# Second product of the expert layer with the activations stationary, in a fused decoder layer

## The chip, the cores and the metric

The kernel runs on one core of a Trainium2 chip. The metric is the device time of one execution in microseconds (us). TensorE is called PE (its weight loads PEld), VectorE DVE, ScalarE ACT, GpSimd POOL and SyncE SP, as in the profile.

## The reference, cut to what matters

The layer takes x of shape (8, 128, 128): 1,024 tokens of width 128. A bidirectional Mamba mixer, a cross attention and a mixture of experts follow one another, each with a residual and a layer norm. All is float32. The change lies in the experts:

```
logits = tokens @ gate_w                       # 8 experts
expert_idx = argmax(softmax(logits))           # top 1
pos = cumsum(one_hot(expert_idx)) - 1          # place in the expert's queue, capacity 160
expert_input = einsum('tec,td->ecd', sec_mask, tokens)     # (8, 160, 128)
h = relu(einsum('ecd,edf->ecf', expert_input, w1))         # (8, 160, 512)
expert_output = einsum('ecf,efd->ecd', h, w2)              # (8, 160, 128)
out = einsum('tec,ecd->td', combine_weights, expert_output)
```

## The kernel before, in words

Every engine has a program of its own, written out by hand, and they meet at semaphores. PE's results go to the 8 PSUM banks of 128 x 512 float32. A list, `plan` (lines 210 to 237), names every result in the order in which PE makes it, with the bank that it goes to; from it come the waits: `to_fill` waits until what stood in the bank was read, `filled` tells that it is full, `to_read` waits for that, `was_read` tells that it was copied out.

The mixer takes the first 240 us or so, attention the next 75. The experts are the last stage. POOL writes each token row to its slot in DRAM (`dispatched_tokens`, line 475, 8 indirect transfers), SP loads the 1,280 slots back as `xe` (lines 355 and 356), PE turns them to `xeT` (width on partitions, slots along the row; line 994, carried out in the helper `turn`, line 687), ACT and DVE copy that out of PSUM. Then comes the loop over 8 experts with 160 slots each, in steps `e` of PE's program (lines 997 to 1018):

- `h{e}`: the first product, 4 matmuls of 128 x 160 with a block of w1 stationary and the slots of `xeT` moving (line 1002). It fills a pair of banks, 0 and 1 or 2 and 3. ACT copies it out with a relu, to `hid`, two buffers in turn (line 680); before that it waits until the second product has read the buffer (line 678).
- `eoT{e-1}`: the second product of the expert before, 4 matmuls accumulated over the 512 hidden units with a block of w2 stationary and `hid` moving, 160 columns (line 1010). The result has the width on partitions. It goes to bank 4 or 5; DVE copies it to `eoT` (line 1293, in the helper of line 1032).
- `eo{e-2}`: two transposes of 80 slots each (line 1017, helper line 687) put the slots on partitions: 80 x 2 x 128, in bank 6 or 7. DVE copies that to `eo` (line 1296, the same helper).

SP stores `eo` to DRAM in pairs of experts once both are copied (line 362). POOL waits for all four stores and fetches each token's row with 8 indirect transfers (line 481); DVE weighs it, adds the residual and normalizes (lines 1301, 1174, 1175, 1180), and SP stores the output.

A float32 matmul has two LDWEIGHTS and two MATMUL records in the trace, a transpose one of each.

Of the kernel before, what the change touches and what calls it, by code (L numbers as in the profile page):

```python
# [22 lines left out]
def decoder_layer_kernel(nc, x, ctx_1024, in_proj_w, conv_w, conv_bias, x_proj_w, dt_proj_w, dt_proj_bias,  # L23
                         A_log, D_skip, convb_w, convb_bias, x_proj_b_w, dt_proj_b_w, dt_proj_b_bias,
                         A_b_log, D_b_skip, out_proj_w, Wq, Wk, Wv, Wo, gate_w, w1, w2, out):
    B, S, D = x.shape
# [25 lines left out]
    E = gate_w.shape[1]  # L52
    F = w1.shape[2]
    FC = F // P
    CAP = 160
    HC = CAP // 2
# [9 lines left out]
    with ExitStack() as ctx:  # L66
        def sb(name, shape, dt=F32):
            return ctx.enter_context(nc.sbuf_tensor(name, shape, dt))
# [25 lines left out]
        w2_sb = sb("w2_sb", [P, E, FC, D])  # L94
# [20 lines left out]
        arena = sb("arena", [P, 12, T])  # L115
# [47 lines left out]
        x2T = arena[:, 9, :]  # L163
        xe = arena[:, 0:2, :].rearrange("p a t -> p (a t)")[:, 0:SLOTS].rearrange("p (j d) -> p j d", j=ST)
        xeT = arena[:, 2:4, :].rearrange("p a t -> p (a t)")[:, 0:SLOTS]
        eoT = [arena[:, 9, CAP * k:CAP * k + CAP] for k in range(2)]
        hid = [arena[:, 4 + e, 0:FC * CAP].rearrange("p (c s) -> p c s", c=FC) for e in range(2)]
        eo = arena[:, 6:8, :].rearrange("p a (e s d) -> p (a e) s d", s=2, d=D)
        back = arena[:, 10, :].rearrange("p (b d) -> p b d", b=B)
# [40 lines left out]
        plan = [("xT0", 0), ("xT1", 1), ("winT", 2), ("wkT0", 3), ("xi0", 5), ("xi1", 6), ("xproj", 7), ("dtw", 2)]  # L210
# [20 lines left out]
                plan += [("x2T0", 0), ("logits0", 1)]  # L231
        plan += [("count0", 2), ("x2T1", 3), ("logits1", 4), ("count1", 5)]
        plan += [("xeT0", 0), ("xeT1", 1), ("xeT2", 2)]
        for e in range(E + 2):
            plan += [(f"h{e}", 2 * (e % 2), 2)] if e < E else []
            plan += [(f"eoT{e - 1}", 4 + (e - 1) % 2)] if 1 <= e <= E else []
            plan += [(f"eo{e - 2}", 6 + e % 2)] if e >= 2 else []
        where, before, holder, uses = {}, {}, [None] * 8, [0] * 8
        for n, (name, i, *width) in enumerate(plan):
            if n == scan_from:  # L240
# [8 lines left out]
        def wait_read(eng, name):  # L249

            i, n = where[name]
            eng.wait_ge(read[i], n + 1)

        def to_fill(pe, name):

            for old in before[name]:
                wait_read(pe, old)
            return bank[:, where[name][0], :]

        def filled(name, last):  # L260
            last.then_inc(full[where[name][0]], 1)

        def to_read(eng, name):

            i, n = where[name]
            eng.wait_ge(full[i], n + 1)
            return bank[:, i, :]

        def was_read(name, last):
            last.then_inc(read[where[name][0]], 1)  # L270
# [7 lines left out]
        def half(th):  # L278
            return slice(TH * th, TH * th + TH)

        def group(g):
            return slice(HB * g, HB * g + HB)
# [32 lines left out]
        def _(sp):  # L315
# [5 lines left out]
            for dr in range(2):  # L321
                _, cb, xp, _, _, _, dsk = mamba_in[dr]
                for v, vec in ((dr, cb), (2 + dr, dsk)):
                    sp.dma_start(vec_rows[NH * v:NH * v + NH, :],
                                 vec.rearrange("(h p) -> h p", p=P)).then_inc(small_in, 16)
                sp.dma_start(xproj[:, dr, :], xp).then_inc(small_in, 16)
# [160 lines left out]
        def _(sc):  # L487
# [134 lines left out]
            for g in range(2):  # L622
# [3 lines left out]
                for j in range(GH):  # L626
                    last = sc.activation(k_maskT[:, group(g), j, :], src, ACT.Copy, scale=head_mask[:, j:j + 1])
# [7 lines left out]
            for g in range(2, HEADS // GH):  # L635
                last = sc.activation(q_maskT[:, g, half(0)], src, ACT.Copy, scale=group_mask[:, g:g + 1])
# [8 lines left out]
            for i in range(LAST):  # L645
                if i < 2 * B:
                    wait_read(sc, f"s{i}")
                    for h in range(CH):
                        last = sc.activation(prob[i % 3][:, h, :], prob[i % 3][:, h, :], ACT.Exp, scale=SCALE,  # L649
                                             accum_out=rsum[:, i % 3, h:h + 1])  # L650
                    last.then_inc(exp_ok, 1)
                if 2 <= i < 2 * B + 2:
                    c = i - 2
# [21 lines left out]
            for e in range(E):  # L675
                to_read(sc, f"h{e}")
                if e >= 2:
                    to_read(sc, f"eoT{e - 2}")
                i = where[f"h{e}"][0]
                was_read(f"h{e}", sc.activation(  # L680
                    hid[e % 2], bank[:, i:i + 2, :].rearrange("p a (c s) -> p (a c) s", c=2)[:, :, 0:CAP], ACT.Relu))
# [3 lines left out]
        def _(pe):  # L685
            def turn(dst, src):
                return pe.transpose(dst, src, ident[0:src.shape[0], 0:src.shape[0]])  # L687
# [42 lines left out]
            dst = to_fill(pe, "xproj")  # L730
# [65 lines left out]
            dst = to_fill(pe, "skip")  # L796
# [69 lines left out]
            for g in range(2):  # L866
                for h in range(NH):
                    wait_read(pe, f"yT{h}{g}")
                dst = to_fill(pe, f"o{g}")
                for b in range(HB):  # L870
                    t0 = TH * g + S * b
                    for h in range(NH):
                        last = pe.matmul(dst[:, D * b:D * b + D], yzT[:, h, t0:t0 + S], woutT[:, h, :],
                                         start=(h == 0), stop=(h == NH - 1))
# [12 lines left out]
            for g in range(2):  # L887
                wait_read(pe, f"ctxT{g}")
                dst = to_fill(pe, f"k{g}")
                filled(f"k{g}", pe.matmul(dst, qkvT[:, 1, :], ctxT[:, half(g)], start=True, stop=True))  # L890
                dst = to_fill(pe, f"v{g}")
                for b in range(HB):
                    t0 = TH * g + S * b
                    last = pe.matmul(dst[:, D * b:D * b + D], ctxT[:, t0:t0 + S], qkvT[:, 2, :],
                                     start=True, stop=True)
# [73 lines left out]
            for i in range(LAST):  # L969
# [6 lines left out]
                if i % 2 == 1 and 5 <= i < 2 * B + 5:  # L976
                    b = i // 2 - 2
                    wait_read(pe, f"av{b}")
                    dst = to_fill(pe, f"wo{b}")
                    for g in range(HEADS // GH):  # L980
                        last = pe.matmul(dst[:, 0:D], outT[b % 2][:, S * g:S * g + S], woT[:, g, :],  # L981
                                         start=(g == 0), stop=(g == HEADS // GH - 1))
# [11 lines left out]
                turn_group(f"xeT{g}", [xe[:, j, :] for j in range(4 * g, min(4 * g + 4, ST))])  # L994
            for g in range(3):
                wait_read(pe, f"xeT{g}")
            for e in range(E + 2):
                if e < E:
                    to_fill(pe, f"h{e}")
                    for c in range(FC):  # L1000
                        at = (BANK // 2) * (c % 2)
                        last = pe.matmul(bank[:, where[f"h{e}"][0] + c // 2, at:at + CAP],  # L1002
                                         w1_sb[:, e, P * c:P * c + P], xeT[:, CAP * e:CAP * e + CAP],
                                         start=True, stop=True)
                    filled(f"h{e}", last)
                if 1 <= e <= E:
                    wait_read(pe, f"h{e - 1}")
                    dst = to_fill(pe, f"eoT{e - 1}")
                    for c in range(FC):
                        last = pe.matmul(dst[:, 0:CAP], w2_sb[:, e - 1, c, :], hid[(e - 1) % 2][:, c, :],  # L1010
                                         start=(c == 0), stop=(c == FC - 1))
                    filled(f"eoT{e - 1}", last)
                if e >= 2:
                    wait_read(pe, f"eoT{e - 2}")
                    dst = to_fill(pe, f"eo{e - 2}")
                    for s in range(2):
                        last = turn(dst[0:HC, D * s:D * s + D], eoT[e % 2][:, HC * s:HC * s + HC])
                    filled(f"eo{e - 2}", last)


        @block.vector
        def _(ve):
# [8 lines left out]
            def evacuate(name, dst, rearranged=lambda ap: ap):  # L1031
                was_read(name, ve.tensor_copy(dst, rearranged(to_read(ve, name))))  # L1032
# [69 lines left out]
            def add_log(h):  # L1102

                _, rest = soft[0][h]
                for th in range(2):
                    wait_read(ve, f"d0{h}{th}")
                ve.wait_ge(log_ok, h + 1)
                ve.tensor_tensor(delta[:, 0, h, :], delta[:, 0, h, :], rest, ALU.add).then_inc(delta_ok, 1)
# [45 lines left out]
            for g in range(STEPS):  # L1154
                for i in range(4):
# [3 lines left out]
                    k = 4 * g + i  # L1159
# [126 lines left out]


            evacuate("xeT1", xeT[:, BANK:2 * BANK])
            for e in range(E + 1):
                if e < E:  # L1290
                    if e >= 2:
                        to_read(ve, f"eo{e - 2}")
                    evacuate(f"eoT{e}", eoT[e % 2], lambda ap: ap[:, 0:CAP])
                if e == 0:
                    continue
                evacuate(f"eo{e - 1}", eo[0:HC, e - 1, :, :], lambda ap: ap[0:HC, 0:2 * D].rearrange("p (s d) -> p s d", s=2))


            for b in range(B):
# [33 lines left out]
```

## Time and profile before

| | |
|---|---|
| time, median of 3 runs | 387.41 us (386.73 to 387.95) |
| the profiled execution's own time | 386.72 us |
| its span, first to last instruction | 384.8 us |
| PE, busy share of the span | 79% |
| DVE | 76% |
| ACT | 70% |
| POOL | 59% |
| mean granted clock of PE | 0.918 of full speed |

Times in the views are counted from the start of the span. A busy share is a mean over stages with different limits, so what one edit is worth is read from the stage that it lies in. The chain of waits is the series of pieces, each of which was released by the one before, that ends with the last instruction. A granted clock of 1.00 is TensorE's level of 2.4 GHz, 0.50 that of 1.2 GHz.

### The profile page before, as it was taken

To read this page: it belongs to the slowest core of one execution; us is meant where nothing else is said; L and a number is where in the kernel's file an instruction comes from. 1 tells how busy PE (TensorE), PEld (TensorE's weight loads), DVE (VectorE), ACT (ScalarE), POOL (GpSimd) and SP (SyncE) were. 2 spreads that over 40 slices of the span, in tenths; PEclk is the share of its full clock that TensorE was granted. 3 is DMA by queue.
4 is the path that set the end of the run, shared out by engine and by line. 5 is a ranking of instruction groups with operands and counts; after the bars stand their busy time and mean duration, and the time that the engine had idled before them with its cause. 6 is when DMAs were issued, how large, how long until landed. Compare 5 with 4: busy or idle time off the path is not lost.

```text
span 384.8 us, 5604 instructions
## 1 busy us (share of the span) xinstructions
PE 305.1 (79%) x1688; PEld 188.0 (49%) x1688; DVE 291.4 (76%) x462; ACT 268.4 (70%) x682; POOL 228.2 (59%) x148
## 2 busy tenths in 40 slices
PE   4999507999999998999999999788999764089700
PEld 3443305555566554554554558335666553079600
DVE  2849788999999999999999967697777636102335
ACT  3589766999999988999999964598999941022100
POOL 7500817999999988889888721154454534400063
PEclk9999855999999999999999999999999997559955
DMA  6986211133233332223330000000000000210212
GB/s 159 306 248 219 61 55 52 59 110 104 62 113 106 112 109 97 83 96 111 109 110 2 1 0 3 1 0 3 0 2 1 3 2 14 71 40 17 53 41 68
DMA packets 16770, 26.92 MB, mean 70 GB/s; under 512 B 1965, under 2 KB 10309, under 8 KB 16741
## 3 DMA queue, kind: packets, MB, share of 16 engines
q1 hardware_dynamic: 16036, 25.46, 21.2%
q0 software_dynamic: 704, 1.10, 1.0%
q8 instruction: 14, 0.23, 0.2%
q14 instruction: 16, 0.12, 0.1%
HBM read 24.00 MB, written 2.56 MB: 69 GB/s over the span
## 4 chain that ended last, share of the span: by engine, by line
PE 34%; DVE 31%; issue 10%; POOL 10%; ACT 9%; DMA 4%; SPq 0%; DVEq 0%; POOLq 0%; ACTq 0%
DVE arena L1127 20%; PE bank L687 12%; POOL arena L441 5%; PE bank L908 5%; DVE acc L1137 3%; PE bank L1002 3%; ACT arena L649 2%; PE bank L1010 2%; PE bank L825 2%; PE bank L981 2%; PE bank L747 2%; POOL dispatched_tokens L475 2%; PE bank L725 2%; POOL arena L481 2%; PE bank L927 2%
## 5 line engine op out<-in xcount | busy, mean ns | idle before, releaser
L441 POOL TENSOR_TENSOR arena<-arena,k_maskT 128x1024 f32<-128x1024 f32 x64 | 150.9, 2382 | 42.0 <-DVE arena L1114 21.5
L1127 DVE TENSOR_TENSOR_SCAN arena<-bank,arena 128x512 f32<-128x512 f32 x128 | 146.3, 1206 | 0.9 <-ACT bank L578 0.9
L687 PE MATMUL bank<-ident,arena 128*128 128x128 f32 (+1 forms) x686 | 102.2, 286 | 42.8 <-DVE arena L1127 23.5
L687 PEld LDWEIGHTS bank<-ident,arena 128*128 128x128 f32 (+1 forms) x686 | 77.2, 144 | 107.4 <-DVE arena L1127 69.9
L578 ACT ACTIVATE bank<-delta,a_neg 128x508 f32<-128x508 f32 x128 | 88.4, 692 | 10.1 <-DVE arena L1127 6.4
L825 PE MATMUL bank<-conv_in_T,ident 128*128 128x512 f32 x192 | 93.7, 598 | 0.0
L589 ACT ACTIVATE conv_in_T<-bank,c_col 128x256 f32<-128x256 f32 x192 | 80.3, 472 | 11.4 <-PE bank L687 10.6
L467 POOL TENSOR_TENSOR arena<-arena,rsum 128x1024 f32<-128x1024 f32 x16 | 30.4, 1897 | 36.9 <-DVE rsum L1219 36.9
L649 ACT ACTIVATE arena<-arena 128x128 f32<-128x128 f32 x128 | 37.7, 295 | 7.0 <-DVE arena L1214 6.8
L825 PEld LDWEIGHTS bank<-conv_in_T,ident 128*128 128x128 f32 x192 | 31.8, 192 | 15.8 <-issue 15.0
L1032 DVE COPY arena<-bank 128x160 f32<-128x160 f32 (+2 forms) x20 | 8.1, 433 | 33.3 <-PE bank L1010 17.6
L908 PE MATMUL bank<-k_maskT,uT 128*128 128x512 f32 x64 | 30.9, 607 | 1.4 <-DVE uT L1198 0.8
L1213 DVE TENSOR_REDUCE rmax<-bank 128x8 f32<-128x1024 f32 x16 | 19.5, 1217 | 12.8 <-PE bank L687 7.0
L1137 DVE SCALAR_TENSOR_TENSOR acc<-bank,c_col,acc 128x256 f32<-128x256 f32 x64 | 27.6, 475 | 1.5 <-PE bank L687 1.1
L481 POOL DMA_INDIRECT arena<-expert_outputs,take_u x8 | 7.6, 951 | 35.5 <-DMA expert_outputs<-arena 33.4
L489 ACT ACTIVATE arena<-bank 128x512 f32<-128x512 f32 (+1 forms) x18 | 10.3, 578 | 21.4 <-PE bank L687 18.7
L649 ACT ACTIVATION_READ_ACCUMULATOR arena<-arena 128x1 f32 x128 | 23.9, 187 | 0.0
L1214 DVE TENSOR_TENSOR arena<-bank,rmax 128x1024 f32<-128x1024 f32 x16 | 19.6, 1224 | 0.6
L660 ACT ACTIVATE arena<-bank 128x1024 f32<-128x1024 f32 x16 | 16.1, 1003 | 2.0 <-PE bank L687 2.0
L908 PEld LDWEIGHTS bank<-k_maskT,uT 128*128 128x128 f32 x64 | 11.0, 190 | 12.6 <-issue 10.1
L680 ACT ACTIVATE arena<-bank 128x640 f32<-128x640 f32 x8 | 5.6, 704 | 14.4 <-PE bank L1002 14.4
L453 POOL TENSOR_SCALAR rstd<-moments 128x4 f32<-128x4 f32 x6 | 1.4, 235 | 22.2 <-DVE moments L1175 22.1
(161 smaller groups left out, 343.3 us busy)
## 6 DMA issues: line engine op xcount, KB each, us to landing
k_maskT<-b_rows SPq DMA_DIRECT2D x32, 512.0 KB, 3.7
w_sb<-in_L_ffn_w SPq DMA_DIRECT2D x1, 2048.0 KB, 11.2
dispatched_tokens<-zeros SPq DMA_DIRECT2D x1, 640.0 KB, 16.4
expert_outputs<-arena SPq DMA_DIRECT2D x4, 160.0 KB, 2.1
x_tok<-in_x SPq DMA_DIRECT2D x1, 512.0 KB, 3.9
ctx_tok<-in_ctx SPq DMA_DIRECT2D x1, 512.0 KB, 4.1
out<-arena SPq DMA_DIRECT2D x2, 256.0 KB, 2.3
arena<-dispatched_tokens SPq DMA_DIRECT2D x1, 384.0 KB, 3.8
```

The source lines that it names most:

```text
L441: gp.tensor_tensor(dBx[g % 2][h], du[:, dr, h, :], b_bc[:, g % RING, :], ALU.mult).then_inc(dBx_ok, 1)
L467: gp.tensor_tensor(prob[i % 3], prob[i % 3], rsum[:, i % 3, :].unsqueeze(2).to_broadcast([P, CH, S]), ALU.mult).then_inc(prob_ok, 1)
L578: sc.activation(tiles(bank[:, k % DA_BANKS, :], HB)[:, :, inner], tiles(delta[:, dr, h, half(q)], HB)[:, :, inner], ACT.Exp, scale=a_neg[: ...
L589: sc.activation(y_part[:, p, at:at + DI], hT(g, b), ACT.Copy, scale=c_col[:, dr, b, n:n + 1]).then_inc(part_ok, 1)
L649: last = sc.activation(prob[i % 3][:, h, :], prob[i % 3][:, h, :], ACT.Exp, scale=SCALE, accum_out=rsum[:, i % 3, h:h + 1])
L687: return pe.transpose(dst, src, ident[0:src.shape[0], 0:src.shape[0]])
L825: last = pe.matmul(bank[:, Y_BANK + p, :], ident[:, :], y_part[:, p, :], start=(g == 0), stop=False, skip_group_check=True)
L908: last = pe.matmul(bank[:, g, :], q_maskT[:, g, S * b:S * b + S], k_maskT[:, b, :, :].rearrange("p j k -> p (j k)"), start=True, stop=True)
L1127: ve.tensor_tensor_scan(o, a, v, 0.0, ALU.mult, ALU.add).then_inc(scanned, 1)
L1137: ve.scalar_tensor_tensor(acc[:, b, :], hT(g, b), c_col[:, dr, b, n:n + 1], acc[:, b, :], ALU.mult, ALU.add).then_inc(acc_ok, 1)
L1213: link(ve.tensor_reduce(rmax[:, c, :], src, AX.X, ALU.max))
L1214: was_read(f"s{i}", ve.tensor_tensor(prob[i % 3], src, rmax[:, c, :].unsqueeze(2).to_broadcast([P, CH, S]), ALU.subtract))
```

## The change

The second product swaps its operands. The stationary one is now a block of `hid`, 128 hidden units by 80 slots, the moving one a block of w2, 128 hidden units by the 128 columns of the width. For each of the two halves of 80 slots, 4 such matmuls accumulate, so an expert takes 8 of them, and the result stands with the slots on partitions at once: 80 x 2 x 128 in one bank. The transposes, the tile `eoT` and DVE's copy into it are gone; DVE copies `eo` alone. The results go to banks 4 to 7 in turn. ACT waits on `eo{e-2}` before it writes `hid` again. PE's loop has one step fewer.

```diff
-        eoT = [arena[:, 9, CAP * k:CAP * k + CAP] for k in range(2)]
...
-        for e in range(E + 2):
+        for e in range(E + 1):
             plan += [(f"h{e}", 2 * (e % 2), 2)] if e < E else []
-            plan += [(f"eoT{e - 1}", 4 + (e - 1) % 2)] if 1 <= e <= E else []
-            plan += [(f"eo{e - 2}", 6 + e % 2)] if e >= 2 else []
+            plan += [(f"eo{e - 1}", 4 + e % 4)] if e >= 1 else []
...
                 if e >= 2:
-                    to_read(sc, f"eoT{e - 2}")
+                    to_read(sc, f"eo{e - 2}")
...
-            for e in range(E + 2):
+            for e in range(E + 1):
...
-                if 1 <= e <= E:
+                if e >= 1:
                     wait_read(pe, f"h{e - 1}")
-                    dst = to_fill(pe, f"eoT{e - 1}")
-                    for c in range(FC):
-                        last = pe.matmul(dst[:, 0:CAP], w2_sb[:, e - 1, c, :], hid[(e - 1) % 2][:, c, :],
-                                         start=(c == 0), stop=(c == FC - 1))
-                    filled(f"eoT{e - 1}", last)
-                if e >= 2:
-                    wait_read(pe, f"eoT{e - 2}")
-                    dst = to_fill(pe, f"eo{e - 2}")
+                    dst = to_fill(pe, f"eo{e - 1}")
                     for s in range(2):
-                        last = turn(dst[0:HC, D * s:D * s + D], eoT[e % 2][:, HC * s:HC * s + HC])
-                    filled(f"eo{e - 2}", last)
+                        for c in range(FC):
+                            last = pe.matmul(dst[0:HC, D * s:D * s + D], hid[(e - 1) % 2][:, c, HC * s:HC * s + HC],
+                                             w2_sb[:, e - 1, c, :], start=(c == 0), stop=(c == FC - 1))
+                    filled(f"eo{e - 1}", last)
...
-            for e in range(E + 1):
-                if e < E:
-                    if e >= 2:
-                        to_read(ve, f"eo{e - 2}")
-                    evacuate(f"eoT{e}", eoT[e % 2], lambda ap: ap[:, 0:CAP])
-                if e == 0:
-                    continue
-                evacuate(f"eo{e - 1}", eo[0:HC, e - 1, :, :], lambda ap: ap[0:HC, 0:2 * D].rearrange("p (s d) -> p s d", s=2))
+            for e in range(E):
+                evacuate(f"eo{e}", eo[0:HC, e, :, :], lambda ap: ap[0:HC, 0:2 * D].rearrange("p (s d) -> p s d", s=2))
```

What moves on PE is shown by the instructions in their order, first of the program before, from the transposes of `xe` to the third expert. `w_sb` stands for w1 or w2, `arena` for the buffer that holds `xe`, `xeT`, `hid`, `eoT` and `eo`; the shape is that of the result.

```order
L687 MATMUL bank<-ident,arena 128x128 x10
L1002 MATMUL bank<-arena,w_sb 128x160 x8
L1010 MATMUL bank<-arena,w_sb 128x160 x4
L1002 MATMUL bank<-arena,w_sb 128x160 x4
L1010 MATMUL bank<-arena,w_sb 128x160 x4
L687 MATMUL bank<-ident,arena 80x128 x2
```

The same place after the change (all lines lie 2 lower, the second product is now line 1009):

```order
L685 MATMUL bank<-ident,arena 128x128 x10
L1000 MATMUL bank<-arena,w_sb 128x160 x8
L1009 MATMUL bank<-w_sb,arena 80x128 x8
L1000 MATMUL bank<-arena,w_sb 128x160 x4
L1009 MATMUL bank<-w_sb,arena 80x128 x8
L1000 MATMUL bank<-arena,w_sb 128x160 x4
```

The second product has 8 matmuls of 80 x 128 in the place of 4 of 128 x 160, and no transposes come between. The end of PE's program, before:

```order
L1002 MATMUL bank<-arena,w_sb 128x160 x4
L1010 MATMUL bank<-arena,w_sb 128x160 x4
L687 MATMUL bank<-ident,arena 80x128 x2
L1010 MATMUL bank<-arena,w_sb 128x160 x4
L687 MATMUL bank<-ident,arena 80x128 x4
L66 UNCONDITIONAL_BRANCH
```

And after:

```order
L1009 MATMUL bank<-w_sb,arena 80x128 x8
L1000 MATMUL bank<-arena,w_sb 128x160 x4
L1009 MATMUL bank<-w_sb,arena 80x128 x16
L66 UNCONDITIONAL_BRANCH
```

After the last first product come 16 matmuls, the second products of the last two experts, and PE is done; the last pair of transposes, which waited for DVE's copy of `eoT7`, is gone.

## Rows read from the trace of the kernel before

**Rows 1.** The page: busy time by engine, and the granted clock in 40 slices.

```profile
PE 305.1 (79%) x1688; PEld 188.0 (49%) x1688; DVE 291.4 (76%) x462; ACT 268.4 (70%) x682; POOL 228.2 (59%) x148
...
PEclk9999855999999999999999999999999997559955
```

**Rows 2.** Chain of waits, end of the experts: start us, length us, what.

```profile
358.48 0.22 PE bank L687 x2
358.70 1.09 PE bank L1002 x8
359.79 1.09 PE bank L1010 x8
360.88 0.22 PE bank L687 x2
361.10 1.10 PE bank L1010 x8
...
362.29 0.34 DVE arena L1032
...
362.67 0.43 PE bank L687 x2
...
363.13 0.43 DVE arena L1032
...
363.62 2.04 DMA expert_outputs<-arena
...
366.44 0.99 POOL arena L481
```

**Rows 3.** PE by stretches: stretch, its length, PE busy (instructions), granted clock, DMA share, GB/s.

```profile
340.70:345.15 4.45, 4.40 (x17) 0.50 0.02 4
345.15:346.57 1.42, 1.42 (x10) 0.76 0.00 0
346.57:348.96 2.39, 2.39 (x20) 1.00 0.00 0
348.96:361.10 12.14, 12.14 (x94) 1.00 0.11 28
```

**Rows 4.** Timeline of PE, first experts: start us, length us, instructions in order.

```profile
345.15 1.58 PE L1010 MATMUL bank<-arena,w_sb 128*128 128x160 f32 x8
346.57 1.25 PE L1002 MATMUL bank<-arena,w_sb 128*128 128x160 f32 x8
347.66 1.25 PE L1010 MATMUL bank<-arena,w_sb 128*128 128x160 f32 x8
348.74 0.38 PE L687 MATMUL bank<-ident,arena 128*80 128x128 f32 x2
348.96 1.25 PE L1002 MATMUL bank<-arena,w_sb 128*128 128x160 f32 x8
```

**Rows 5.** Groups by form, experts' stage: count, busy us, mean ns; idle before, releaser.

```profile
L1010 PEld LDWEIGHTS bank<-arena,w_sb 128*128 128x128 f32 x64 | 9.6, 198 | 0.0
L680 ACT ACTIVATE arena<-bank 128x640 f32<-128x640 f32 x8 | 5.6, 704 | 14.4 <-PE bank L1002 14.4
L1032 DVE COPY arena<-bank 80x256 f32<-80x256 f32 x8 | 3.3, 411 | 0.2 <-PE bank L687 0.2
L1032 DVE COPY arena<-bank 128x160 f32<-128x160 f32 x8 | 2.6, 325 | 17.6 <-PE bank L1010 17.6
```

**Rows 6.** Timeline of PE: transposes and float32 matmuls of 128 moving columns.

```profile
232.48 1.04 PE L687 MATMUL bank<-ident,ctx_tok 128*128 128x128 f32 x8
233.35 3.74 PE L873 MATMUL bank<-woutT,uT 128*128 128x128 f32 x32
236.92 1.02 PE L890 MATMUL bank<-arena,qkvT 128*128 128x512 f32 x2
```

**Rows 7.** Groups by form, output product of the mixer: the mean of one record.

```profile
L873 PE MATMUL bank<-woutT,uT 128*128 128x128 f32 x32 | 3.7, 275 | 0.0
```

**Rows 8.** Timeline of PE, attention: products with 32 stationary columns, then the next.

```profile
267.79 0.64 PE L927 MATMUL bank<-arena,delta 128*32 128x128 f32 x16
268.36 1.16 PE L981 MATMUL bank<-woT,arena 128*128 128x128 f32 x8
```

## Prediction

> **What bounds the kernel now.** I read the page first. PE is busy 79% of the span and has the most records, but its granted clock dips near the end [rows 1], so the last stage must be read by itself. The chain of waits does that. From the first product of the experts (340.75 us) to the last copy of `eo` it is made of PE's instructions alone, one straight after the other, until the very last expert, where DVE's copy of `eoT7` and a pair of transposes stand by themselves [rows 2]. PE's rows by stretch say the same: 12.14 us busy out of 12.14, at clock 1.00 [rows 3]. ACT's relu copy takes 0.704 us of each expert's 2.40 and DVE's two copies 0.325 + 0.411 = 0.74; ACT waited 14.4 us for PE's first product and DVE 17.6 us for its second [rows 5]. In this stage, then, PE's issue time is the time, and copies are free except the last ones. What follows hangs on the last copy: the last store is issued at 363.62, and only when it has landed does POOL fetch rows, at 366.44 [rows 2]. A shift in PE's end shifts everything behind it.
>
> A record's duration (299 or 275 ns) is not its cost, since records overlap. The cost is the distance from start to start. One period of the loop: first product at 346.57, second at 347.66, transposes at 348.74, next first product at 348.96 [rows 4]. That is 1.09 + 1.08 + 0.22 us: 8 records of 160 moving columns at 136 ns each, and 2 transposes at 110 ns each.
>
> **The change, part by part.**
>
> *Removed on PE.* (a) Seven second products at full clock, 7 x 1.085 = 7.60 us, and the first one, 345.15 to 346.57, 1.42 us; this one straddles the rise of the clock, since its granted clock is 0.76 against 0.50 in the stretch ahead of it and 1.00 in the one after [rows 3, 4]. A mean of 0.76 over 1.42 us means 0.68 us at the lower level. (b) Seven pairs of transposes on the way, 7 x 0.22 = 1.54 us. (c) The tail: the chain has the end of `eoT7` at 362.20 and that of the last transposes at 363.10 [rows 2], so 0.90 us; of this about 0.16 us is only the overlap that the last record of every series shows, so some 0.85 us. Sum removed: 11.4 us. (The same as 363.10 - 345.15 = 17.95, less the six first products that stay, 6 x 1.09 = 6.54.)
>
> *Added on PE.* 8 matmuls of 128 moving columns per expert, 16 records. What does one cost, with 80 stationary columns? No row of before shows exactly this. The nearest from below is the transpose with the same 80 columns, 110 ns [rows 4]; transposes with 128 stationary columns come at (233.35 - 232.48)/8 = 109 ns, so the width of what is loaded made no difference there. The nearest from above is the mixer's output product, real float32 matmuls of 128 columns that accumulate, 32 records in 236.92 - 233.35 = 3.57 us: 112 ns [rows 6]. I take 110: 16 x 0.110 = 1.76 us per expert, where 1.085 + 0.22 = 1.31 stood. Seven experts: 12.32 us. The first one has 0.68 us at the lower clock, in which three records fit at 0.22 us, then 13 at 0.110: 2.11 us. At the end the last record lasts 0.275 us rather than its spacing [rows 7], 0.16 us more. Sum added: 14.6 us. Balance: +3.2 us (+3.0 with 109 ns, +3.4 with 112).
>
> The count of columns says why: before, an expert's second product moved 4 x 160 columns, twice, plus 2 x 128 for the transposes, 1,536 in all; now it moves 8 x 128, twice, 2,048. The change saves the transposes and pays for them by using only 80 of the 128 columns of the array.
>
> *Weighed against the skill.* The row says that 128 moving columns cost 109 to 112 ns whether 80 or 128 columns are loaded, and that 160 cost 136 with 128 loaded: the pace goes by what moves. The Trainium skill, "TensorE: Matmul & The Clock Gate", section "LDWEIGHTS (loading the stationary operand)", has the load's time go by its columns, 128 columns in some 107 ns and 80, as an estimate from its formula, in 67; were loads the limit, by those figures the sum would come to 16 x 0.067 = 1.07 us per expert and a gain of about 2 us. The transposes of 80 columns at 110 ns speak against that.
>
> *Nothing, while the cover stands.* DVE's eight copies of `eoT` (0.325 us each) lay beside PE's work but for the last, which is in (c). The copies of `eo` keep their shape, 80 x 256 and 0.411 us [rows 5], and only the last counts, as before. ACT's relu of `h{e}` must be done before `eo{e}` begins; between them PE now has `eo{e-1}`, 1.76 us, against 0.70 us of relu, so the cover grows from 1.09. Before the last second product it is the same. Without that cover each expert would pay 0.7 us. ACT's new wait, for `eo{e-2}` before it writes `hid`, is met: PE has finished it before `h{e}` is even started. Its queue behind that wait holds only the next relu. Four banks in turn mean that `eo{e}` waits for the copy of `eo{e-4}`, four periods old. SP's stores are issued as before, behind the second copy of a pair; the period grows from 2.4 to 2.85 us, so three of the four stores have more room, and the last keeps its distance from PE's end. Up to 345.15 us the two programs are alike, the ten transposes of `xe` and two first products, so the clock should rise at the same moment. If it rose only after the first new product, that would add about 1.4 us: 13 records at 0.22 in place of 0.11.
>
> **Sum.** 386.72 + 3.2 = 389.9 us for the profiled execution; that one lies at the low end of the three runs, 0.7 below their median, so on the median I expect 387.41 + 3.2 = 390.6 us, 0.8% slower. A measurement of this kernel can tell about 0.3%, 1.2 us, from no change.
>
> **The rivals.**
>
> *The load sets the pace, and no change is seen.* Suppose the 136 ns of the second product before were the time of a 128-column load; with 80 columns it would be 136 x 80/128 = 85 ns. Then 16 x 0.085 = 1.36 us against 1.31: 128 records at 25 ns less than I took, -3.2, and the balance is zero, 387.4 us. For it: loads show 190 to 198 ns each and are always under way [rows 5]. Against it: 112 ns in rows 6 with 128 columns loaded, 110 ns with 80. Chance 5%. This is the same rule of the skill as above, with a pace from rows; 85 ns is also the point below which the change would be a gain.
>
> *Faster: the two halves overlap in the array.* The products of attention with 32 stationary columns come at (268.36 - 267.79)/16 = 36 ns a record [rows 8]; there, four heads in turn write to four different strips of 32 partitions. If the products of 80 columns overlapped like that even in part, say at 70 ns, 16 records would take 1.12 us, and the time would be 387.4 - 1.9 = 385.5 us; at 36 ns far less. It decides below 85 ns a record. Against it: all eight matmuls write to partitions 0 to 79, so no two are on different strips, and the transposes of 80 columns, which also lie side by side in one bank, did not overlap. Chance 3%.
>
> *Slower still: loads no longer hide.* Twice as many stationary blocks come per column moved. If a load of 80 columns, or a switch of the accumulating group, held a record to 136 ns, as with 160 columns before, it is 128 x 0.026 = 3.3 us on top: 393.9 us. For it: the first load of a series shows 190 ns. Against: 112 ns with 128-column loads under the same pattern. Chance 7%.
>
> *It saves nothing because nothing was on the path.* That the removed transposes and copies were hidden anyway, and the new matmuls too, would leave 387.4; but the chain shows PE unbroken, so this has its part in the 5% above.
>
> **How the numbers follow.** The forecast, PE-bound with 109 to 112 ns a record, has 85%, with 390.6 us. Its own spread is +3.0 to +3.4 for the spacing, up to 1.4 for the clock's rise, and 0.7 us either way for the run, which gives 389.3 to 392.1. The range 389.1 to 392.3 leaves out the cases at 393.9, 387.4 and 385.5. Slower by over 0.3%: 85 + 7 = 92%; within 0.3%: 5%; faster: 3%.
>
> **What the profile after should show.** The second product as 16 records per expert, starts 109 to 112 ns apart; first product to first product 2.83 to 2.88 us instead of 2.40; PE with 1,736 records; no transposes and no copy of 128x160 in this stage; DVE's copies 80 x 256 with long idle time before them; no idle time of PE from 340.7 to some 366.2; the last store issued near 366.8 instead of 363.62; all ahead of 345.15 and all behind the last store unchanged. I am wrong if the spacing is under 100 or over 120 ns, if PE waits for ACT between the last two second products, or if the clock leaves 1.00 in the loop.

## The result and the profile after

| | before | changed |
|---|---|---|
| median of 6 runs | 387.32 us | 390.31 us |
| the profiled execution | 386.72 us | 389.87 us |
| its span | 384.8 us | 387.9 us |

The ratio is 1.0087, 95% interval 1.0059 to 1.0116: 0.9% slower. The forecast was 390.6 us, range 389.1 to 392.3. A second timing, 12 executions of the changed kernel and 23 of the one before, gave 390.17 against 387.68 us, ratio 1.0064 (1.0041 to 1.0086).

The page of the changed kernel, busy time by engine and the granted clock, against [rows 1]:

```profile
PE 308.4 (80%) x1736; PEld 191.8 (49%) x1736; DVE 289.6 (75%) x454; ACT 268.4 (69%) x682; POOL 228.3 (59%) x148
...
PEclk9999856999999999999999999999999995569955
```

PE has 48 more records and 3.3 us more busy time; DVE has 8 copies fewer. The chain of waits, end of the experts (start us, length us, what), against [rows 2]:

```profile
340.70 4.61 PE bank L1000 x16
345.31 2.05 PE bank L1009 x16
347.36 1.09 PE bank L1000 x8
348.45 1.75 PE bank L1009 x16
...
361.54 1.09 PE bank L1000 x8
362.63 3.51 PE bank L1009 x32
...
366.16 0.43 DVE arena L1025
...
366.65 2.04 DMA expert_outputs<-arena
...
369.48 0.98 POOL arena L479
```

From 340.70 to 366.14 us there is nothing but PE, and what follows the last copy has the lengths that it had. The last store went out at 363.62 us before, at 366.65 now: 3.03 us later. The timeline of PE shows the new period, against [rows 4]:

```profile
345.10 2.26 PE L1009 MATMUL bank<-w_sb,arena 128*80 128x128 f32 x16
347.20 1.25 PE L1000 MATMUL bank<-arena,w_sb 128*128 128x160 f32 x8
348.29 1.91 PE L1009 MATMUL bank<-w_sb,arena 128*80 128x128 f32 x16
350.03 1.25 PE L1000 MATMUL bank<-arena,w_sb 128*128 128x160 f32 x8
```

From start to start: first product 1.09 us, second product 350.03 - 348.29 = 1.74 us, 16 records of 109 ns; period 2.83 us instead of 2.40. The groups by form of the experts' stage answer to [rows 5]:

```profile
L1009 PE MATMUL bank<-w_sb,arena 128*80 128x128 f32 x128 | 15.5, 276 | 0.0
L1009 PEld LDWEIGHTS bank<-w_sb,arena 128*80 128x80 f32 x128 | 14.9, 154 | 0.0
...
L678 ACT ACTIVATE arena<-bank 128x640 f32<-128x640 f32 x8 | 5.6, 703 | 17.2 <-PE bank L1000 17.2
L1025 DVE COPY arena<-bank 80x256 f32<-80x256 f32 x8 | 3.4, 421 | 22.8 <-PE bank L1009 22.8
```

PE never idles ahead of the second product (0.0), ACT and DVE wait longer for PE than before (17.2 us for 14.4, 22.8 for 17.6 + 0.2), and DVE's copies of 128 x 160 are gone.

### The profile page after: what moved, and what is told of

It reads as the page before. It is cut to its first block, busy times and chain, and to the rows that moved or that the text cites. A ratio compares the mean times of both kernels' runs of the same rounds, so it can differ in the third digit from the quotient of the medians.

```text
span 387.9 us, 5678 instructions
## 1 busy us (share of the span) xinstructions
PE 308.4 (80%) x1736; PEld 191.8 (49%) x1736; DVE 289.6 (75%) x454; ACT 268.4 (69%) x682; POOL 228.3 (59%) x148
## 4 chain that ended last, share of the span: by engine, by line
PE 36%; DVE 30%; issue 10%; POOL 9%; ACT 9%; DMA 4%; SPq 0%; POOLq 0%; DVEq 0%; ACTq 0%
DVE arena L1120 20%; PE bank L685 13%; PE bank L906 5%; POOL arena L439 5%; PE bank L1009 4%; PE bank L1000 3%; DVE acc L1130 3%; ACT arena L647 2%; PE bank L823 2%; PE bank L979 2%; PE bank L745 2%; POOL dispatched_tokens L473 2%; PE bank L723 2%; POOL arena L479 2%; PE bank L925 2%
## 5 line engine op out<-in xcount | busy, mean ns | idle before, releaser
L685 PE MATMUL bank<-ident,arena 128*128 128x128 f32 x670 | 99.1, 286 | 42.5 <-DVE arena L1120 23.5
L685 PEld LDWEIGHTS bank<-ident,arena 128*128 128x128 f32 x670 | 75.4, 144 | 106.6 <-DVE arena L1120 69.9
L1025 DVE COPY arena<-bank 80x256 f32<-80x256 f32 (+1 forms) x12 | 6.1, 511 | 38.3 <-PE bank L1009 22.8
L678 ACT ACTIVATE arena<-bank 128x640 f32<-128x640 f32 x8 | 5.6, 703 | 17.2 <-PE bank L1000 17.2
L1009 PE MATMUL bank<-w_sb,arena 128*80 128x128 f32 x128 | 15.5, 276 | 0.0
```

Of the source, the lines that this page charges most:

```text
L1009: last = pe.matmul(dst[0:HC, D * s:D * s + D], hid[(e - 1) % 2][:, c, HC * s:HC * s + HC], w2_sb[:, e - 1, c, :], start=(c == 0), stop=(c ...
```

## Experiments

The question left by the prediction was what sets the time of a record: the columns that move (theory M) or those that are loaded (theory L), and so whether the products that the change brought in could be had for less.

**128 stationary columns instead of 80.**

```diff
-  pe.matmul(dst[0:HC, D * s:D * s + D], hid[(e - 1) % 2][:, c, HC * s:HC * s + HC],
+  pe.matmul(dst[0:P, D * s:D * s + D], hid[(e - 1) % 2][:, c, 32 * s:32 * s + P],
```

> The changed kernel with stationary blocks of 128 slots instead of 80 (slots 0 to 127 and 32 to 159, all written to 128 partitions; the copies still take 80 of them, so the halves hold other slots than they should for the second half). Same number of matmuls, same 128 moving columns. Theory M (the pace goes by moving columns): a record every 109 to 112 ns, time within 0.4 us of the changed kernel's 390.3. Theory L (the pace goes by the columns loaded): 109 x 128/80 = 175 ns, 128 records x 66 ns = 8.4 us more, about 398.7.

One execution took 391.02 us, the kernel before on the same chip 386.87. The timeline of PE:

```profile
351.13 1.25 PE L1000 MATMUL bank<-arena,w_sb 128*128 128x160 f32 x8
352.22 1.95 PE L1009 MATMUL bank<-w_sb,arena 128*128 128x128 f32 x16
354.01 0.71 PE L1000 MATMUL bank<-arena,w_sb 128*128 128x160 f32 x4
```

(354.01 - 352.22)/16 = 112 ns, far from 175: M. It is also the 112 ns of the mixer's product [rows 6], which the forecast had kept as its upper end: 3 ns more than with 80 columns. Only the number of loaded columns was changed, and with it the partitions written. The time lies 0.7 us above the changed kernel's 390.3, where I had 0.4 at most: 128 records at 3 ns are 0.4 us, and the first of the second products took 2.57 us instead of 2.10, at a granted clock of 0.68 instead of 0.83.

**40 stationary columns.** The edit is the same with `HC // 2` columns.

> The changed kernel with stationary blocks of 40 slots instead of 80; half of the slots of every expert are left out. Theory M: still 109 ns a record, about 390.3 us. Theory L: 55 ns a record, 7.0 us less, about 383.3.

392.86 us, slower than both theories have it:

```profile
351.78 1.35 PE L1000 MATMUL bank<-arena,w_sb 128*128 128x160 f32 x8
353.06 1.94 PE L1009 MATMUL bank<-w_sb,arena 128*40 128x128 f32 x16
354.93 0.40 PE L1000 MATMUL bank<-arena,w_sb 128*128 128x160 f32 x1
...
365.68 3.69 PE L1009 MATMUL bank<-w_sb,arena 128*40 128x128 f32 x32
```

The last line holds the records of two experts in a row: its 16 further ones take 3.69 - 1.94 = 1.75 us, 109 ns each, as with 80 columns. What grew is the change from one kind of product to the other: the first product now takes 1.28 us to the next start instead of 1.09, the second 1.87 instead of 1.74. The groups of weight loads over six periods (347 to 366 us) show where:

```profile
L1009 PEld LDWEIGHTS bank<-w_sb,arena 128*40 128x40 f32 x95 | 10.2, 119 | 1.1 <-issue 1.0
L1000 PEld LDWEIGHTS bank<-arena,w_sb 128*128 128x128 f32 x48 | 6.7, 189 | 1.1 <-issue 1.1
```

Loads stood idle 2.2 us in these periods; with 80 columns both groups have 0.0. Behind 40 columns the first load of 128 starts together with the first record of its product, at 354.93; behind 80 columns it starts 0.10 us ahead of it, at 349.93 for 350.03. L falls as the pace, since a record did not get cheaper; beyond M there is a cost at each change between 128 and 40 loaded columns, 0.32 us for the two changes of a period. PE's stretch, from 341.54 to 369.38, is 2.40 us longer than the changed kernel's: the changes from the third first product to the last series make 1.8 us of it, and 0.4 us lies in the first of the second products, at a granted clock of 0.72 instead of 0.83. Why a change costs time these runs don't say.

**64 moving columns.** `dst[0:HC, D * s:D * s + D // 2]` and `w2_sb[:, e - 1, c, 0:D // 2]`.

> The changed kernel with 64 moving columns instead of 128; half of the expert output's width is left out. Theory M: 55 to 57 ns a record, 128 x 0.053 = 6.8 us less, about 383.5. Theory L: 109 ns as before, 390.3. If a load of 80 columns has a floor of its own, the spacing shows it: anything between 57 and 109 ns is the time of the load, and PE's records tell it.

385.37 us. The timeline of PE:

```profile
349.27 1.30 PE L1000 MATMUL bank<-arena,w_sb 128*128 128x160 f32 x8
350.41 1.29 PE L1009 MATMUL bank<-w_sb,arena 128*80 128x64 f32 x16
351.54 0.63 PE L1000 MATMUL bank<-arena,w_sb 128*128 128x160 f32 x3
```

(351.54 - 350.41)/16 = 71 ns, between 57 and 109, and 128 x 38 ns = 4.9 us less than 390.3 is the time measured: what moves is no longer the limit. I read the 71 ns as the load of 80 columns. With the 112 ns of 128 columns above this gives a rule for the products of this kernel: a float32 record takes the longer of its moving time (109 ns for 128 columns, 136 for 160) and its load (71 ns for 80 columns, 112 for 128). So L holds as a floor. The changed kernel lies above its floor by 38 ns a record, and M decides there. The rule fits all these spacings, but it isn't tested further: at 64 moving columns the load was not varied, and no product loads 128 columns and moves fewer than 128. It does not carry over to transposes: with 128 columns loaded they come at 109 ns [rows 6], below the 112. Eight smaller ones in the kernel before, with 128 columns loaded on 32 partitions and 32 moving, start 61 or 62 ns apart once under way, at a granted clock of 1.00:

```profile
35.31 0.68 PE L754 MATMUL bank<-ident,rows 32*128 32x32 f32 x8
```

The Trainium skill, "TensorE: Matmul & The Clock Gate", section "LDWEIGHTS (loading the stationary operand)", has a formula for the time of a load by its columns, from which I estimate 67 and 107 ns for these two. As a floor of the products the two runs agree within 5 ns; for the pace of the changed kernel, and for these transposes, it does not hold.

**Two banks in turn.** `4 + e % 4` became `4 + e % 2`.

> The changed kernel with the results of the second product in two banks in turn instead of four. Theory: the copy of an expert's result takes 0.42 us and the bank is wanted again two periods of 2.83 us later, so nothing waits: 390.3 us within 0.4. Rival (the four banks hide a wait): PE idles for DVE once per expert, visible as idle time ahead of the second product, some 0.4 us each, 3 us in all.

389.71 us. The timeline of PE, and behind it the groups of DVE, in the experts' stage:

```profile
350.09 1.25 PE L1000 MATMUL bank<-arena,w_sb 128*128 128x160 f32 x8
351.18 1.91 PE L1009 MATMUL bank<-w_sb,arena 128*80 128x128 f32 x16
352.93 0.84 PE L1000 MATMUL bank<-arena,w_sb 128*128 128x160 f32 x5
```

```profile
L1025 DVE COPY arena<-bank 80x256 f32<-80x256 f32 x8 | 3.4, 421 | 23.0 <-PE bank L1009 23.0
```

The period is 2.84 us with two banks too, and PE never waits for DVE there: the four banks of the change are worth nothing. The single time lies 0.6 us below 390.3, where I had 0.4 at most.

**The new form for the last expert alone**, in the kernel before.

```diff
+                if e == E:
+                    wait_read(pe, f"h{e - 1}")
+                    last_half(0)
-                if 1 <= e <= E:
+                if 1 <= e < E:
...
+                if e == E + 1:
+                    filled(f"eo{E - 1}", last_half(1))
-                if e >= 2:
+                elif e >= 2:
```

> The kernel before, with the new form for the last expert alone (its first half ahead of the transposes of the expert before it, its second half at the very end). Removed: 8 records of 136 ns, and the tail with its wait for the copy, 0.85 us. Added: 16 records of 109 ns and 0.16 us for the end of the last one. 1.745 + 0.16 - 1.09 - 0.85 = 0.0 us: PE ends as far from its start, 22.3 us, as in the kernel before, time 386.9 to 387.4 us. Rival (the tail is worth much more than 0.85 us, or nothing): PE's stretch 0.4 us or more shorter, or 0.8 longer.

One execution took 388.41 us; the kernel before had a median of 387.47 in 13 executions there, spread from 386.89 to 389.07. It is 1.0 us above the 387.4 expected, but in its profile the experts' first product starts at 342.34 us instead of 340.75, so the surplus arose ahead of the edited part, and PE's stretch is what counts:

```profile
361.08 1.25 PE L1020 MATMUL bank<-arena,w_sb 128*128 128x160 f32 x8
362.16 0.38 PE L687 MATMUL bank<-ident,arena 128*80 128x128 f32 x2
362.38 1.04 PE L1000 MATMUL bank<-w_sb,arena 128*80 128x128 f32 x8
363.25 0.38 PE L687 MATMUL bank<-ident,arena 128*80 128x128 f32 x2
363.47 1.04 PE L1000 MATMUL bank<-w_sb,arena 128*80 128x128 f32 x8
```

From the transposes of expert 5 to PE's end it is 364.51 - 362.16 = 2.35 us; in the kernel before, 363.10 - 360.71 = 2.39 (the pair before the last `eoT` starts at 360.71). The tail with its wait was worth what the last expert's longer product costs, within 0.04 us of the sum.

**Blocks of 128 slots, and strips of 32.** Both forms so far leave something unused: with the weights stationary 160 columns move, with 80 slots stationary 48 of the array's 128 columns are empty. The attention's products write to four strips of 32 partitions in turn and come at 36 ns a record [rows 8]. So, cut to the products:

```diff
-                    for s in range(2):
-                        for c in range(FC):
-                            last = pe.matmul(dst[0:HC, D * s:D * s + D], hid[(e - 1) % 2][:, c, HC * s:HC * s + HC], ...
+                    for c in range(FC):
+                        last = pe.matmul(dst[:, 0:D], hid[(e - 1) % 4][:, c, 0:P], w2_sb[:, e - 1, c, :], ...
+                if e in (4, 8):
+                    dst = to_fill(pe, f"rest{(e - 4) // 4}")
+                    for c in range(FC):
+                        for j in range(4):
+                            last = pe.matmul(dst[REST * j:REST * j + REST, 0:D], hid[j][:, c, P:CAP],
+                                             w2_sb[:, e - 4 + j, c, :], ...
```

> A new form of the second product with the activations stationary: slots 0 to 127 of each expert as one block of 128 columns (4 matmuls), and the last 32 slots of four experts as four blocks of 32 columns, each on its own strip of 32 output partitions, with consecutive matmuls on different strips; four hid buffers, and stores of 128 rows plus four stores of 32 rows for each group of four experts. If products on different strips overlap as those of the attention do (36 ns a record in the profile of before): per expert 8 x 0.110 + 8 x 0.036 = 1.17 us against 1.31 before the change and 1.745 after it; with the last wait for the copy gone too, PE ends 1.2 to 1.7 us earlier than before the change, the last copy is 0.1 us shorter, and the small stores may cost up to 1 us: 385.7 to 387.4 us. If they don't overlap (109 ns): 1.745 us per expert as in the changed kernel, about 390.3 us.

> The changed kernel once more, unaltered, timed beside the form with strips: 390.3 us within 0.8, ratio 1.008 to 1.009.

The form with strips took 386.34 us (12 executions), within the expected range, and the kernel before 387.68 (23), ratio 0.9967 (0.9935 to 0.9998). The changed kernel's ratio beside it was 1.0064, under the 1.008 expected, though 1.008 lies within its interval. The timeline of PE in the form with strips and, in the second fence, its chain at the end:

```profile
352.68 1.05 PE L1018 MATMUL bank<-w_sb,arena 128*128 128x128 f32 x8
353.67 1.08 PE L1025 MATMUL bank<-w_sb,arena 128*32 128x128 f32 x32
354.68 1.35 PE L1010 MATMUL bank<-arena,w_sb 128*128 128x160 f32 x8
```

```profile
363.02 0.30 DVE arena L1042
...
363.34 0.32 SPq L368
...
363.70 0.42 SPq L368
...
364.17 0.42 SPq L368
...
364.63 1.50 DMA expert_outputs<-arena
```

The 32 records of four experts take 354.68 - 353.67 = 1.01 us with the change back to wide loads, 32 ns each. Read one by one, the records start in rounds of four, one for each strip: three steps of 6 or 7 ns and then one of 89, so a round takes 109 ns (the first one 133). That is the pace of a single record of 128 moving columns; theory M holds for each strip by itself, and four of them share a round. PE's stretch, 363.00 - 341.54 = 21.46 us, is 0.9 us shorter than the 22.35 of the kernel before, where I had 1.2 to 1.7; the first of the second products ran at a granted clock of 0.50 throughout and took 1.70 us. Behind the last copy the four small stores are issued one after the other: 1.3 us on the path, where I had up to 1.

**The same with one strip in a row.** The loops over `c` and `j` are swapped.

> The form with strips with the matmuls of 32 slots in another order: the four of one expert (one strip) in a row, then the next expert's. Same work. If the overlap comes from different strips, it is lost: 109 ns a record instead of 26, 32 x 0.083 = 2.7 us for each of the two groups, 5.3 us in all, about 391.7 us. If it comes from the 32 columns alone, nothing changes: 386.3.

389.49 us, 3.2 us more than the form with strips. PE's timeline:

```profile
353.50 2.46 PE L1025 MATMUL bank<-w_sb,arena 128*32 128x128 f32 x32
355.89 0.40 PE L1010 MATMUL bank<-arena,w_sb 128*128 128x160 f32 x1
```

2.39 us instead of 1.01; the two groups make 2 x 1.38 = 2.8 of the 3.2 us, and the rest is within what single executions differ by. The overlap hangs on the order of the strips, as expected, but it is not lost altogether: I had 109 ns a record, it is 75. Read one by one, the records at the beginning and at the end start 109 ns apart. Around each border between strips there are four pairs of starts, 6 and 103 ns or 30 and 79 ns apart, and a pair takes the same 109. The trace doesn't name a record's strip, but this fits the last four records of one strip running beside the first four of the next: three borders take 12 of the 32 steps away, and 20 steps of 109 ns are 2.2 us. The rival, that 32 columns are enough, falls.

**The strips ahead of the last block, ScalarE issuing two of the stores.**

```diff
+            plan += [(f"rest{(e - 4) // 4}", 7)] if e in (4, 8) else []
             plan += [(f"eo{e - 1}", 4 + e % 3)] if e >= 1 else []
-            plan += [(f"rest{(e - 4) // 4}", 7)] if e in (4, 8) else []
...
+            store_rest(sc, 1, range(2, 4))
```

> The form with strips, with the products of 32 slots of a group of four experts ahead of the fourth expert's block of 128, so that the last piece of PE's work is a block of 128 and the small stores go out beside it; of the last four small stores ScalarE issues two. In the form with strips the four small stores were issued one after the other, 1.27 us between the end of the last copy and the last issue. Expected: that time goes, one more switch from 32 to 128 loaded columns comes in (0.2 us), so 1.0 us less than the form with strips: 385.3 us, 0.5% under the kernel before. Rival: the small stores still hold the last one back on SP's queue, and nothing is gained (386.3).

385.42 us (8 executions) against 387.47 (13), ratio 0.9942 (0.9922 to 0.9961): 0.6% faster than the kernel before and about 5 us faster than the changed one. The end of the chain:

```profile
359.98 1.01 PE bank L1023 x32
360.99 1.10 PE bank L1030 x8
...
362.12 0.30 DVE arena L1046
...
362.50 1.82 DMA expert_outputs<-arena
```

From the end of the last copy to the landing it is now 364.32 - 362.42 = 1.90 us; it was 366.13 - 363.32 = 2.81 in the form with strips, 0.91 more.

## Why the prediction was right

**Bound by PE in this stage.** Right. The chain is PE alone, idle time ahead of the second product is 0.0, and what PE issues more came back in the time: PE's stretch from the first product to its end is 25.44 us against 22.35, 3.09 more, and the medians differ by 2.99, those of the second timing by 2.49.

**The record of 128 columns.** Taken at 110 ns from a span of 109 to 112; it is 109. The nearest row was the transpose with the same 80 columns loaded, and the run with 128 stationary columns says why the other end did not apply: the 112 ns go with a load of 128 columns, which 80 don't have. The prediction took the transposes as a sign that the width of the load makes no difference; for the products it makes 3 ns. Per expert 1.74 us where the sum had 1.76.

**The first product of the second kind.** 2.11 us forecast, 347.20 - 345.10 = 2.10 measured, with part of it at the lower clock. That the clock rose at the same place was luck: in the second profile of the same kernel this product took 347.33 - 345.06 = 2.27 us.

**The tail.** Priced at 0.85 us removed and 0.16 added. The experiment on the last expert alone agrees within 0.05 us.

**The range.** It does not come out of the terms given for it. Added up, they reach from 387.41 + 3.0 - 0.7 = 389.7 us to 387.41 + 3.4 + 1.4 + 0.7 = 392.9; the prediction has 389.3 to 392.1. The 390.31 measured lies inside both, so nothing hung on it here.

**The costs put at nothing.** ACT's relu, DVE's copies of `eo` and the banks: PE waits for none of them in the profile after, and two banks do as well as four.

**The rivals.** That the load sets the pace was wrong for this shape but right in kind, as a floor 38 ns below. That the two halves overlap did not come about at 80 columns; the mechanism is real where strips differ. Loads that no longer hide did not appear at 80 columns either; something like it did at 40, where records kept their 109 ns and each change of width cost time.

In short, the change removed 256 column passes of transposes per expert and added 768 of products on the engine that was the bound, and relieved an engine that was waiting.

## What to carry to other kernels

Count for each form what the bound engine must issue: in float32 here a matmul costs two records, each the longer of its moving time and its load, whether its stationary block fills 128, 80 or 40 of the array's columns. Which operand to make stationary follows from that count, and a copy saved on an idle engine doesn't enter it. A remainder of 32 columns was cheap when consecutive records went to four different strips, 1.01 us for 32 of them; with each strip's records in a row it was 2.39.

## What the runs showed that I had not expected

- The products have a floor that goes with the loaded columns, 71 ns a record for 80 and 112 for 128. It is hidden under 109 ns of moving with 80 columns and under 136 with 128; at 64 moving columns it is the limit.
- Four strips share the 109 ns that one record of 128 moving columns takes; the 36 ns a record of the attention [rows 8] and the 32 ns of the strips are a quarter of that, 27 ns, and the changes of width.
- Going between 128 and 40 loaded columns and back costs 0.32 us; between 128 and 80 nothing. In the forms with strips the starts on either side of a group of 32 columns lie 0.1 us further apart too.
- The granted clock of this stage does not rise at the same place in every run, though the instructions up to there are alike. With 128 stationary columns the first two products ran at 0.50 throughout and the next stretch still at 0.68; with the strips ahead of the last block the clock rose within the first two products. By stretches, of the first and then of the second kernel (PE busy, PEld, DVE, ACT, POOL, then the granted clock):

```profile
341.29:345.69 4.40, 4.40 (x16) 4.40 (x17) 0.00 (x0) 0.70 (x1) 0.00 (x0) 0.50 0.01 4
345.69:348.26 2.57, 2.57 (x17) 2.57 (x17) 0.00 (x0) 0.70 (x1) 0.00 (x0) 0.68 0.00 0
```

```profile
342.21:345.84 3.63, 3.63 (x16) 3.63 (x17) 0.00 (x0) 0.70 (x1) 0.00 (x0) 0.61 0.02 5
```

The two first products took 3.63 us in the one and 4.40 in the other. Single profiles of this kernel can differ by that and more, and it should not be put down to an edit. The lead of the last form over the one before it is therefore read from the medians, 386.34 - 385.42 = 0.92 us. That fits the 0.91 us that the stores gave back, but the two were timed at different times, and each against its own timing of the kernel before the lead is 2.05 - 1.34 = 0.7 us; a part of it may also be the clock.
